# Two graph layers over 200,000 edges: messages, gather signals and sums by the pair of tiles

## The reference, cut to what matters

```python
x_t  = mlp2(x, W1n, b1n, W2n, b2n)                 # leaky_relu, slope 0.1
e_t  = mlp2(edge_attr, W1e, b1e, W2e, b2e)         # [200000, 32] -> 64 -> 64
agg  = segment_sum(x_t[src] * e_t * dp_scale, dst, 12500)
y    = layernorm(x + agg * res_w) * gamma + beta
x    = layernorm(x + y)
rel_w = einsum('rb,bio->rio', w_comp, weight)      # 8 relations, [64, 64] each
xw    = einsum('ni,rio->rno', x, rel_w)
out   = relu(segment_sum(xw[edge_type, src] * edge_weight, dst, 12500) + h_bias)
x     = layernorm(x + out)
```

## Time and profile before

| | before |
|---|---|
| median of 3 runs | 4970.07 us (4955.96 to 4988.68) |
| the profiled execution | 4952.68 us |
| its span on the core | 4950.8 us |
| mean granted clock of TensorE | 0.664 |
| busy: POOL, PE, DVE, ACT | 60%, 45%, 33%, 7% |
| first gather, last gather of layer 0 | 73.14 us, 2570 us |
| first and last gather of layer 1 | 2671 us, 4909 us |

### The profile page before, as it was taken

One profiled execution on the slowest core, in us unless ns is written; L12 is line 12 of the kernel. 1 busy time (PEld: TensorE's weight loads), 2 busy tenths in 40 slices (PEclk: granted clock), 3 DMA queues, 4 the chain that ended last, 5 costly groups with the idle time before them and its releaser, 6 DMA issues.

```text
span 4950.8 us, 32349 instructions
## 1 busy us (share of the span) xinstructions
PE 2223.0 (45%) x6997; PEld 1406.5 (28%) x6998; DVE 1644.3 (33%) x3785; ACT 324.7 (7%) x686; POOL 2989.6 (60%) x3218
## 2 busy tenths in 40 slices
PE   5555555556556656565665222332322333323333
PEld 5333333333333333333332111121211222212222
DVE  4233333333333334343442122322322233223333
ACT  2000000001111111110111000000000000000000
POOL 6566665656565555555543676666666666666664
PEclk8677777777777777777775555555555556555565
DMA  4111111111111111111111111111111111111111
GB/s 102 30 32 33 33 32 43 32 42 43 42 43 41 37 42 42 42 52 42 51 38 39 23 25 23 22 24 24 24 25 24 25 24 27 25 25 25 24 28 21
DMA packets 199560, 169.74 MB, mean 34 GB/s; under 512 B 82780, under 2 KB 135152, under 8 KB 199250
## 3 DMA queue, kind: packets, MB, share of 16 engines
q0 software_dynamic: 100032, 102.60, 11.0%
q1 hardware_dynamic: 98930, 64.45, 4.3%
q10 hardware_dynamic: 288, 0.07, 0.0%
HBM read 134.80 MB, written 32.10 MB: 34 GB/s over the span
## 4 chain that ended last, share of the span: by engine, by line
another core or an unknown queue 43%; issue 27%; DVE 11%; PE 10%; DVEq 5%; ACT 1%; ACTq 1%; POOL 1%; DMA 0%; SPq 0%; POOLq 0%
DVE acc L1008 3%; PE ps_agg L1388 3%; DVE work L1088 3%; DVE work L997 2%; PE ps_fin L1477 2%; PE ps_z L1364 1%; DVEq L987 1%; PE ps_o L1380 1%; POOL rows L595 1%; DVEq L1022 1%; DVEq L1008 1%; PE ps_agg L1477 1%; ACT low L656 1%; DVEq L997 1%
## 5 line engine op out<-in xcount | busy, mean ns | idle before, releaser
L595 POOL DMA_INDIRECT rows<-node_table,acc x1523 | 1437.9, 944 | 1009.9 <-DVE work L1088 556.9
L595 POOL DMA_INDIRECT rows<-rel_table,row_ix x1563 | 1476.8, 945 | 861.7 <-issue 480.5
L1388 PE MATMUL ps_agg<-work 128*128 128x256 f32 x2348 | 895.2, 529 | 1520.5 <-DVE work L1088 1080.9
L1388 PEld LDWEIGHTS ps_agg<-work 128*128 128x128 f32 x2348 | 582.5, 264 | 1855.1 <-DVE work L1088 1172.4
L1008 DVE TENSOR_TENSOR acc<-acc,ps_agg 64x128 f32 x1174 | 328.9, 280 | 914.6 <-remote 722.0
L1055 DVE SCALAR_TENSOR_TENSOR hid<-ps_z,b1e_c,low 128x512 f32<-128x512 f32 x196 | 147.2, 751 | 1304.0 <-ACT low L656 1041.1
L997 DVE TENSOR_TENSOR work<-ps_x,rel 128x1024 f32<-128x1024 f32 x392 | 479.0, 1222 | 277.6 <-issue 231.3
L1364 PE MATMUL ps_z<-attrT,W1e_d 128*128 128x256 f32 (+1 forms) x784 | 376.3, 613 | 7.4 <-ACT enorm L747 7.4
L1088 DVE TENSOR_TENSOR work<-rows,ps_o 128x256 f32<-128x256 f32 x782 | 323.1, 413 | 78.1 <-DMA rows<-rel_table,row_ix 46.0
L1388 PE MATMUL ps_z<-work 128*128 128x256 f32 x392 | 172.6, 585 | 371.8 <-DVE work L1088 205.6
L1388 PE MATMUL ps_T<-work 128*128 128x256 f32 x388 | 169.3, 582 | 322.0 <-issue 176.3
(11 more groups left out here) (137 smaller groups left out, 1083.7 us busy)
## 6 DMA issues: line engine op xcount, KB each, us to landing
rows<-rel_table,row_ix POOLq DMA_INDIRECT x1563
attr<-in_edge_attr_dram SPq DMA_DIRECT2D x39, 640.0 KB
rows<-node_table,acc POOLq DMA_INDIRECT x1523
rel_table<-acc SPq DMA_DIRECT2D x19, 1280.0 KB
node_table<-work SPq DMA_DIRECT2D x24, 128.0 KB, 2.0
out_dram<-x_sb SPq DMA_DIRECT2D x19, 160.0 KB
x_sb<-in_x_dram SPq DMA_DIRECT2D x1, 768.0 KB, 7.1
acc<-in_dst_dram SPq DMA_DIRECT2D x1, 768.0 KB
```

The costliest lines, as they stand in the source:

```text
L595: nc.gpsimd.indirect_dma_start(rows[0:n, t % BODY, j, :], None, table, bass.IndirectOffsetOnAxis(ap=lists[0:n, t, j : j + 1], axis=0),).th ...
L1388: last = nc.tensor.matmul(bank[:, 0 : 2 * P], data[:, 2 * jj : 2 * jj + 2, :], hot[:, 2 * jj : 2 * jj + 2, :], start=(jj == 0), stop=(jj = ...
```

## The change

1. **Message.** One DVE instruction of 128x512 for a pair instead of two of 128x256. `msg_ready` and `scattered` are one semaphore a layer with one signal a pair, and `gathered` one for each pair of the buffer. POOL waits for the pair's message for both of its tiles.
2. **Sums.** Both tiles' sums lie in the halves of one bank; PE waits once and signals once a pair. Layer 0 always uses `ps_agg0`; layer 1 takes `ps_agg0` and `ps_agg1` in turn.
3. **Order on DVE.** The wait for `mm2_done` stands ahead of the transpose; both adds follow; the one-hot and the whole message come last in layer 0. In layer 1 both adds follow the whole message.
4. **Lists.** POOL multiplies the sources by 8 while it converts them and adds the types (`form_rows`, five instructions at the end of the node steps). PE turns three lists instead of four, ACT copies the relation rows, and DVE gets the sources by a shift to the right by 3.
5. **Besides,** the layer norms' chain has a semaphore for each of its steps, and `rel_products` no longer waits for an add, as its second bank is now `ps_agg1`, which layer 0 leaves free.

```diff
-        ps_xT = ps_T[:, V * P : (V + 1) * P]
-        sums = [[[ps_agg0, ps_agg1], [ps_agg0, ps_agg1]], [[ps_agg0, ps_agg1], [ps_z, ps_T]]]
+        ps_xT = ps_T[:, 0:P]
+        sums = [[ps_agg0, ps_agg0], [ps_agg0, ps_agg1]]
         ps_span = [ps_agg0, ps_agg1]
-        ps_rel = [ps_fin, ps_agg0]
+        ps_rel = [ps_fin, ps_agg1]
...
+        row_banks = [ps_agg0, ps_agg1, ps_T, ps_fin]
...
-        gathered = [[sem(f"gathered{l}_{u}") for u in range(BODY)] for l in range(2)]
+        gathered = [[sem(f"gathered{l}_{u}") for u in range(HALF)] for l in range(2)]
...
-        msg_ready = [[sem(f"msg_ready{l}_{v}") for v in range(V)] for l in range(2)]
+        msg_ready = [sem(f"msg_ready{l}") for l in range(2)]
...
-        scattered = [[sem(f"scattered{l}_{v}") for v in range(V)] for l in range(2)]
+        scattered = [sem(f"scattered{l}") for l in range(2)]
...
-        MM2_LEAD, SUM_LEAD, ADD_LEAD = 1, 2, [2, 3]
+        MM2_LEAD, SUM_LEAD, ADD_LEAD = 1, 2, [[2, 2], [2, 3]]
...
-                nc.gpsimd.tensor_copy(
-                    raw_lists[0:rows_c, n, c, 0:m], int_lists[0:rows_c, n, c, 0:m]
-                ).then_inc(dst_cast if n == DST else lists_cast, 1)
+                o, a = raw_lists[0:rows_c, n, c, 0:m], int_lists[0:rows_c, n, c, 0:m]
+                if n == SRC:
+                    nc.gpsimd.tensor_scalar(o, a, float(R), None, ALU.mult).then_inc(rows_cast, 1)
+                else:
+                    nc.gpsimd.tensor_copy(o, a).then_inc(dst_cast if n == DST else rows_cast, 1)
+            def form_rows(c):
+                pool.wait_ge(rows_cast, RCH + c + 1)
+                rows_c, m = ((P, ST), (R_REST, ST), (1, TAIL_P * J))[max(0, c - RC + 1)]
+                o, a = (raw_lists[0:rows_c, n, c, 0:m] for n in (SRC, TYPE))
+                nc.gpsimd.tensor_tensor(o, o, a, ALU.add).then_inc(rows_formed, 1)
...
+                if CAST_FIRST + 3 * RCH <= q < CAST_FIRST + 4 * RCH:
+                    form_rows(q - CAST_FIRST - 3 * RCH)
...
-                    pool.wait_ge(list_taken, 6)
+                    pool.wait_ge(src_ready, 1)
                 if t >= BODY:
-                    pool.wait_ge(msg_ready[l][t % V], (t - BODY) // V + 1 + MSG_LEAD)
+                    pool.wait_ge(msg_ready[l], (t - BODY) // V + 1 + MSG_LEAD)
...
-                    ).then_inc(gathered[l][t % BODY], 16)
+                    ).then_inc(gathered[l][t // V % HALF], 16)
             for l in range(2):
                 ready, count = ((table_ready, 16 * NODE_STORES), (table2_ready, 16 * (CHUNKS - 1 + REST)))[l]
                 pool.wait_ge(ready, count)
                 if l == 1:
-                    pool.wait_ge(row_taken, 4)
+                    pool.wait_ge(list_taken, 6)
...
-            for n, o in ((SRC, src_turned), (WEIGHT, enorm)):
-                for c, bank in enumerate(list_banks):
-                    act.wait_ge(list_turned, n * 4 + c + 1)
+            for n, (o, banks) in enumerate(((row_ix, row_banks), (enorm, list_banks))):
+                for c, bank in enumerate(banks):
+                    act.wait_ge(list_turned, (n + 1) * 4 + c + 1)
...
-            def row_of(o, sources, types):
-                return nc.vector.scalar_tensor_tensor(o, sources, float(R), types, ALU.mult, ALU.add)
-            for c, bank in enumerate(list_banks):
-                dve.wait_ge(list_turned, TYPE * 4 + c + 1)
...
-                link(row_of(row_ix[:, tiles, :], src_turned[:, tiles, :], turned[:, 0:n, :]))
...
+            dve.wait_ge(list_taken, 6)
+            nc.vector.tensor_scalar(
+                src_turned[:, 0:FULL, :], row_ix[:, 0:FULL, :], R.bit_length() - 1, None, ALU.logical_shift_right)
+            nc.vector.tensor_scalar(
+                src_turned[:, FULL, 0:TAIL_FULL], row_ix[:, FULL, 0:TAIL_FULL], R.bit_length() - 1, None,
+                ALU.logical_shift_right)
...
+            dve.sem_inc(src_ready, 1)
...
-                dve.wait_ge(scattered[l][v], count(p, 0, SUM_LEAD))
-                add_window(window_of(u, v), sums[l][u % 2][v], 0).then_inc(added[l][v], 1)
+                if v == 0:
+                    dve.wait_ge(scattered[l], count(p, 0, SUM_LEAD))
+                else:
+                    dve.wait_ge(added[l][0], count(p, 0, ADD_LEAD[l][0]))
+                add_window(window_of(u, v), sums[l][u % 2], v * 2 * P).then_inc(added[l][v], 1)
...
+                if not is_fixed(p) or p >= 3:
+                    products_of(p - 2)
                 nc.vector.transpose(attrT[:, :], attr[:, u // HALF % 2, u % HALF, :]).then_inc(attr_turned, 1)
-            def message(l, p, u, v):
-                slot = u % HALF * V + v
+            def products_of(p):
+                dve.wait_ge(mm2_done, count(p, 0, MM2_LEAD))
+            def message(l, p, u):
+                slot, n = u % HALF, width(p) * J
                 if is_fixed(p):
-                    of_tile = TILE_GATHERS if p < LAST else 16 * (TAIL_FULL + 1)
-                    dve.wait_ge(gathered[l][slot], p // HALF * TILE_GATHERS + of_tile)
+                    of_pair = PAIR_GATHERS if p < LAST else 16 * (TAIL_FULL + 1)
+                    dve.wait_ge(gathered[l][slot], p // HALF * PAIR_GATHERS + of_pair)
                 else:
                     if slot == 0:
-                        dve.reg_add(landed, landed, TILE_GATHERS)
+                        dve.reg_add(landed, landed, PAIR_GATHERS)
                     dve.wait_ge(gathered[l][slot], landed)
-                tile = rows[:, slot, :, :]
+                tiles = rows[:, slot * V : slot * V + width(p), :, :].rearrange("p t j f -> p (t j) f")
                 if l == 0:
-                    if v == 0:
-                        dve.wait_ge(mm2_done, count(p, 0, MM2_LEAD))
-                    factor = ps_o[u % 2][:, v * J * F : (v + 1) * J * F].rearrange("p (j f) -> p j f", f=F)
+                    factor = ps_o[u % 2][:, 0 : n * F].rearrange("p (j f) -> p j f", f=F)
                 else:
                     if slot == 0 and is_fixed(p):
                         dve.wait_ge(weights_staged, p // HALF + 1)
                     elif slot == 0:
                         dve.reg_add(staged, staged, 1)
                         dve.wait_ge(weights_staged, staged)
-                    factor = ps_o[u // HALF % 2][:, slot * J : (slot + 1) * J].rearrange(
-                        "p (j o) -> p j o", o=1).to_broadcast([P, J, F])
-                nc.vector.tensor_tensor(
-                    msg[:, u % 2, v * J : (v + 1) * J, :], tile, factor, ALU.mult).then_inc(msg_ready[l][v], 1)
+                    factor = ps_o[u // HALF % 2][:, slot * V * J : slot * V * J + n].rearrange(
+                        "p (j o) -> p j o", o=1).to_broadcast([P, n, F])
+                nc.vector.tensor_tensor(msg[:, u % 2, 0:n, :], tiles, factor, ALU.mult).then_inc(msg_ready[l], 1)
...
                 if not is_fixed(p) or p + 2 <= LAST:
                     edge_hidden(p + 2)
-                if not is_fixed(p) or p > 0:
-                    dve.wait_ge(added[0][1], count(p, -1, ADD_LEAD[1]))
-                message(0, p, u, 1)
                 if not is_fixed(p) or p + 3 <= LAST:
                     attr_turn(p + 3, (u + 3) % TURN, i + (u + 3) // TURN)
-                add_sums(0, p, u, 0)
-                dve.wait_ge(added[0][0], count(p, 0, ADD_LEAD[0]))
+                else:
+                    products_of(q)
+                for v in range(V):
+                    add_sums(0, p, u, v)
+                dve.wait_ge(added[0][1], count(p, 0, ADD_LEAD[0][1]))
                 main_one_hot(q, n % 2)
-                message(0, q, n, 0)
-                add_sums(0, p, u, 1)
+                message(0, q, n)
                 extras(0, p, u, i)
                 if not is_fixed(p):
                     dve.reg_add(lead, lead, 1)
...
                 q, n = p + 1, (u + 1) % TURN
                 if not is_fixed(p) or p > 0:
-                    dve.wait_ge(added[1][1], count(p, -1, ADD_LEAD[1]))
+                    dve.wait_ge(added[1][1], count(p, -1, ADD_LEAD[1][1]))
                 main_one_hot(q, n % 2)
-                message(1, q, n, 0)
-                add_sums(1, p, u, 0)
-                dve.wait_ge(added[1][0], count(p, 0, ADD_LEAD[0]))
-                if width(q) == V:
-                    message(1, q, n, 1)
-                add_sums(1, p, u, 1)
+                message(1, q, n)
+                for v in range(V):
+                    add_sums(1, p, u, v)
...
+                    pe.wait_ge(list_taken, 6)
             pe.wait_ge(node_out, PAIRS)
             pe.wait_ge(first_taken, 1)
-            for n in (DST, SRC, TYPE, WEIGHT):
+            for n in (DST, SRC, WEIGHT):
                 if n == WEIGHT:
                     pe.wait_ge(list_loaded[WEIGHT], 16 * 3)
-                elif n != DST:
-                    pe.wait_ge(lists_cast, RCH * n)
+                elif n == SRC:
+                    pe.wait_ge(rows_formed, RCH)
...
-            def sum_by_target(data, hot, bank):
```

(22 more changed lines are left out.)

74 lines of the change are left out of this document (37 added, 37 removed).

## The result

| | before | the change |
|---|---|---|
| median, same chip | 4979.38 us (4955.96 to 4996.13) | 5155.48 us (5149.13 to 5163.48) |
| span of the profiled execution | 4950.8 us | 5153.3 us |

The account below looks back on a forecast made before the run. POOL's gathers were taken as the bound, 10.0 us a pair, plus pauses for late PE signals. From 4952.7 us, prelude -13, layer 0 +45 and layer 1 -142 gave 4843, with 17 for the median 4860 us; range 4660 to 5110 us.

Parts of the forecast that it names:

- Layer 0: Layer 0's new order on DVE: longer pauses of 8.3 us, but each message frees a whole pair; +45 us.
- n: Pairs for each POOL pause in layer 0: chosen as 3 (+45 us), with 4 (-85) and 2 (+308) as bounds.
- the formula: Layer 0's time for a pair: 10.0 us of gathers plus the 8.3 us pause divided by pairs for each pause.
- rival C: Layer 0: third message misses the prompt stretch, two pairs for each pause, 14.15 us a pair, +308 us; chance 0.20.
- The wait for `mm2_done`: Layer 0, DVE: wait moved ahead of the transpose; costs nothing as long as `mm1_done` of the same step is later.
- Layer 1: Layer 1: one PE signal a pair, passing each 10.7 us, so POOL rarely pauses; 10.75 us a pair, -142 us.
- S: Theory in the follow-ups: each late PE signal waits its turn in a queue, about 10 us each while POOL gathers.
- gaps of 20 us: Sign in layer 1: such gaps between two pairs' adds, instead of about 10.7 us, would mean rival B.
- rival B: PE's lateness goes by instructions, not signals: layer 1 gains nothing, layer 0 moves 45 us at most; 4957 to 5002 us; chance 0.26.
- I: Theory in the follow-ups: lateness goes by PE's instructions, about 1.3 us each while POOL gathers, once a stock is used up.
- Prelude: Before the layers: the types' four of eight signals go, shortening POOL's 20.84 us pause; -13 us, gain bounded by 0 to 20.8.
- Half of the 42.6 us: Prelude: half the time between ACT's last copies of sources and first of weights, 21.3 us, taken as basis for the gain.

Follow-up runs that it names:

- Message first: The changed kernel with layer 0's whole message right behind hid, ahead of transpose, adds and one-hot; 1.0005 to 1.001 on prompt chips, 1.0133 with a hold on a late one.
- a1_change_itself: The changed kernel, unaltered, measured again beside the kernel before on a late chip: 5196.07 us against 4967.44, ratio 1.0462.
- the change with the hold: The changed kernel, PE's first layer 0 product of every second pair held for a POOL semaphore, against the kernel before on a late chip: 5114.82 us, 1.0309.
- the three kernels that would show it: Three runs of the kernel before with one matmul call a tile instead of two in layer 1, against the kernel before: 0.9999, 1.0002 and 1.0001.
- e2_signals_doubled: The kernel before with a second, unawaited semaphore raised by each tile's sum, against the kernel before: 1.0002 in both runs, on prompt chips.

## Why the prediction was wrong

*The bound and the lateness.* Right: POOL's gathers took 0.944 to 0.946 us again, the pauses are what moves, and on a prompt chip nothing is left of them. What the prediction could not see is that the signals are late on some chips only. Its sum for a late one failed at two steps.

*Layer 0* is the first step that failed: +45 us forecast, +176 measured. The forecast named the pause (8.3 us; 8.5 measured) and its parts; what was wrong is n, the pairs for each pause. It was chosen as 3, by the times of one cycle of the kernel before. The cycle shown from the calm part has three messages for a rest, but its pause is 9.7 us, with 4.4 instead of 3.0 us until `low`; n is 2.6 over that part and falls just under 2 towards the layer's end. (ACT's work, which is `low` and the chunks', is 113 us there and 64 us at the start, in equal windows, so the chunks' share has grown; that this is the reason was not tested.) Over the layer, 190.4 pairs by 87 pauses make n = 2.19: the formula gives 10.0 + 8.5/2.19 = 13.9 us, 13.7 measured. The baseline was too kind as well, for 103 pauses of 5.4 us are n = 1.85 and not the 2 of the 40 us that were looked at. This is rival C, which decides below n = 2.3. Message first bears out its mechanism, the longer way to the message, by taking most of the loss back. The wait for `mm2_done`, which the sum put at nothing, did cost nothing: the transpose behind it waited 1.5 us in the whole run.

*Layer 1* is the second, and it had the wrong cause: -142 us forecast, +32 measured. The 10.7 us between adds were read as the price of a signal. They could as well be the price of the 4 matmuls and 4 loads behind it, and the rows before the change, with one signal for each eight, cannot tell the two apart. With one signal for sixteen, the median gap went from 10.5 to 21.0 us: 1.3 us for each of these instructions, before and after. It is 21.7 us in a1_change_itself and 21.0 us in the change with the hold. The change itself is thus the test of S, and S fails: half the signals didn't shorten a pair's 21 us. These are the "gaps of 20 us" that the prediction had named as the sign of rival B. That the time goes by the instructions (I), and not by something else that each tile's sums bring along, was argued and not shown: the three kernels that would show it met prompt chips. Why layer 1 lost 32 us, and not nothing, is open too. Rival B had given layer 1 nothing, which was nearly right, and layer 0 at most 45 us, which was not: the result is C in layer 0 and B in layer 1, which no rival had together.

*Prelude*: 13 us forecast, 0.4 us measured. The types' signals are gone, and the weights' come earlier, but not the last one:

```profile
103.41 0.59 ACT L760 COPY enorm<-ps_o 128x512 f32<-128x512 f32 x1 [7.54 <-remote]
...
111.81 0.59 ACT L760 COPY enorm<-ps_o 128x512 f32<-128x512 f32 x1 [7.82 <-remote]
...
122.31 0.59 ACT L760 COPY enorm<-ps_z 128x512 f32<-128x512 f32 x1 [9.91 <-remote]
...
130.73 0.18 ACT L760 COPY enorm<-ps_fin 128x24 f32<-128x24 f32 x1 [7.83 <-remote]
...
143.88 0.94 POOL L610 DMA_INDIRECT rows<-node_table,acc  x1 [18.71 <-DVE work L1107]
```

POOL's first forty gathers ended at 125.2 us and the last part came 5.5 us later; before, all of the weights came at 129.69 us, 6.2 us behind the gathers' end at 123.5. So the last signal came through only once POOL rested, 6.2 us into its rest before and 5.5 us in the change, and the signals that were taken away lay ahead of that, under POOL's own gathers. The way from there to the first message is nearly the same. Half of the 42.6 us was the wrong term for the gain: the last signal ends the wait, and it did not come earlier with fewer signals ahead of it.

*Instruction supply*, the rule named under rival B ("Runtime: NRT & Kernel Launch", "Instruction fetch mechanics", of the Trainium skill): q14 carries 299 packets in the kernel before on a late chip and 299 or 300 in the nearly equal kernels on prompt ones. In the changed kernel itself it carries 279 packets in both measurements on late chips and 280 on the prompt one. Nor is a packet slower: by the traces the median one takes 0.44 us in the kernel before, and 0.47 us in the change on the prompt chip. The same refills stand beside both kinds, which speaks against them as the cause. What makes the signals late on some chips stays open.

## What to carry to other kernels

Where one engine's signal is late and another's buffers run dry, the pause holds the whole way from that signal to the instruction that frees a buffer: put that instruction first, and work that nobody waits for behind it. Before merging signals, look for rows that show that the signal and not the work behind it takes the time; rows in which the two always go together can't. Count events per pause over the whole layer, from the wait view, and don't choose the number from a calm stretch. And compare two kernels on one chip: between chips one kernel differed by more than any of these changes.

## What the runs showed of the hardware

The same program takes 4068 to 4075 us on five chips and 4952 to 4979 us on others, with gathers of 0.943 to 0.947 us on average on both kinds. For the changed kernel, 1015 of the 1087 us between the spans on a late and a prompt chip (5153.3 and 4066.3 us) lie in the windows of the two layers, where POOL waited 1055.6 us for messages on the late chip and 3.4 us on the prompt one. Behind these waits stand PE's signals: one reached ACT 10.3 us after its product's recorded end, 3.0 us into POOL's pause, and on a prompt chip one came at once while POOL gathered. The granted clock doesn't explain it (0.74 and 0.57 in the layers on the late chip, 0.80 and 0.53 in e2_signals_doubled on a prompt one).

Where signals are late, they come in steps of about 0.7 us: of the 41 gaps between late adds in layer 1 of the kernel before, 37 are 9.8, 10.5, 11.2 or 11.9 us. What the step is, no run shows.

A semaphore raised in the program ahead of POOL's wait came only at the end of the wait. In the change with the hold, the gather ahead of it ended at 401.06 us, the raise stands at 406.82 us, and the next gather, after 5.99 us of idle time, at 407.04 us; the pauses that end at 432.00 and 454.04 us show the same. So PE was held until POOL went on, and not until it came to rest.
